# Gated cross-attention block: the context in pairs of tiles, the turn of the probabilities half a step earlier, row sums on ScalarE, side pieces at other places

## The reference, cut to what matters

```
x = x + tanh(g_xattn[0]) * xattn0(layernorm(x), ctx)     # 16 heads of 128, q and k RMS-normalised
x = x + tanh(g_ffn[0])   * mixture0(layernorm(x))        # dense layer and the best 2 of 8 low-rank experts
x = x + tanh(g_xattn[1]) * xattn1(layernorm(x), ctx)     # out = V @ sigmoid(Q^T K / sqrt(64)), Q = x, K = V = ctx
x = x + tanh(g_ffn[1])   * experts1(layernorm(x))        # the best 1 of 8 experts
```

```
q = rms_norm(x @ q_w + q_b, nq_s);  k = rms_norm(ctx @ ki_w + ki_b, nki_s);  v = ctx @ vi_w + vi_b
out = softmax(q k^T / sqrt(128)) v  per head and sequence;   xattn0 = out @ o_w + o_b
```

## Time and profile before

| | us |
|---|---|
| median of 3 runs | 1546.93 (1543.83 to 1551.09) |
| profiled execution, its own time | 1544.57 |
| its span, first to last instruction | 1542.8 |
| PE busy | 1419.3 (92%) |
| DVE busy | 976.3 (63%) |
| ACT busy | 599.5 (39%) |
| POOL busy | 63.8 (4%) |

### The profile page before, as it was taken

The page is one execution under the profiler, slowest core; times in us unless marked ns, Lnnn a source line. Parts: engine busy times, 40 slices in busy tenths (PEclk is TensorE's granted clock), DMA queues, the critical chain, the costliest instruction groups (busy, mean ns, idle before and its releaser), DMA issues.

```text
span 1542.8 us, 28633 instructions
## 1 busy us (share of the span) xinstructions
PE 1419.3 (92%) x10671; PEld 1224.8 (79%) x10671; DVE 976.3 (63%) x3000; ACT 599.5 (39%) x1065; POOL 63.8 (4%) x42
## 2 busy tenths in 40 slices
PE   7799999999999989999999999999899999999666
PEld 7688878788887978888887878879778888879545
DVE  6666677566775568565775667746686557746434
ACT  3344544434344343433434334443434434443221
POOL 2000000100010000100001000000001000000000
PEclk9999999999999999999999999999999999999858
DMA  7211411112112121112112121120211111220000
GB/s 267 76 62 69 151 56 43 69 55 96 42 56 69 42 84 55 58 55 96 56 42 69 55 84 48 64 69 32 94 55 56 55 69 56 69 69 17 25 0 14
DMA packets 48765, 100.31 MB, mean 65 GB/s; under 512 B 7569, under 2 KB 31345, under 8 KB 47985
## 3 DMA queue, kind: packets, MB, share of 16 engines
q1 hardware_dynamic: 48624, 98.38, 18.5%
HBM read 85.78 MB, written 12.58 MB: 64 GB/s over the span
## 4 chain that ended last, share of the span: by engine, by line
PE 67%; DVE 21%; issue 6%; ACT 4%; DMA 0%; SPq 0%; DVEq 0%; ACTq 0%
PE bank L116 44%; PE bank L897 7%; PE bank L999 4%; PE bank L908 3%; PE bank L874 3%; DVE pt L1299 3%; DVE stats L1341 2%; PE bank L888 2%; ACT ao_hi L633 2%; ACT xn L657 1%; DVE rmax L1316 1%; PE bank L1011 1%; PE bank L864 1%; DVE logit L1314 1%; DVE ao_lo L1306 1%
## 5 line engine op out<-in xcount | busy, mean ns | idle before, releaser
L644 ACT ACTIVATE k_sb<-bank,vecs 128x512 f32<-128x512 f32 x128 | 87.9, 687 | 341.2 <-PE bank L116 341.2
L1299 DVE COPY pt<-bank 64x128 f32<-64x128 f32 x512 | 147.4, 288 | 105.8 <-PE bank L888 94.9
L116 PE MATMUL bank<-so,ao_hi 128*128 128x256 f32 x1024 | 198.0, 292 | 2.9 <-DVE ao_lo L1306 2.9
L116 PE MATMUL bank<-sv,ct_hi 128*128 128x256 f32 x1024 | 197.8, 292 | 0.0
L1306 DVE SCALAR_TENSOR_TENSOR ao_lo<-bank,vecs,ao_hi 128x512 fp32r<-128x512 f32 x128 | 96.0, 750 | 151.3 <-ACT ao_hi L633 150.0
L897 PE MATMUL bank<-pt,v_sb 128*128 128x128 f32 x1024 | 140.1, 280 | 32.7 <-DVE pt L1299 32.6
L897 PEld LDWEIGHTS bank<-pt,v_sb 128*128 128x128 f32 x1024 | 127.3, 191 | 52.3 <-DVE pt L1299 41.6
L116 PEld LDWEIGHTS bank<-sv,ct_hi 128*128 128x128 f32 x1024 | 156.2, 189 | 12.8 <-issue 7.8
L116 PEld LDWEIGHTS bank<-so,ao_hi 128*128 128x128 f32 x1024 | 156.5, 190 | 3.3 <-issue 3.3
L116 PE MATMUL bank<-so,ao_lo 128*128 128x256 f32 x512 | 143.6, 280 | 0.0
L116 PE MATMUL bank<-sv,ct_lo 128*128 128x256 f32 x512 | 142.9, 279 | 0.0
(11 more groups left out here) (228 smaller groups left out, 2773.7 us busy)
## 6 DMA issues: line engine op xcount, KB each, us to landing
sv<-v_scratch SPq DMA_DIRECT2D x56, 512.0 KB, 3.2
so<-o_scratch SPq DMA_DIRECT2D x56, 512.0 KB, 3.2
cin<-in_ctx_dram SPq DMA_DIRECT2D x16, 512.0 KB, 4.9
xin<-in_x_dram SPq DMA_DIRECT2D x8, 512.0 KB, 4.9
xres<-in_x_dram SPq DMA_DIRECT2D x8, 512.0 KB, 5.0
v_scratch<-sv SPq DMA_DIRECT2D x8, 512.0 KB, 2.7
o_scratch<-so SPq DMA_DIRECT2D x8, 512.0 KB, 2.6
out_dram<-x SPq DMA_DIRECT2D x8, 512.0 KB, 3.0
```

What stands on the lines that cost most here:

```text
L116: last = pe.matmul(out, lhs[a], rhs[b], start=start and n == 0, stop=stop and n == 2, **kw)
L644: act.activation(k_sb[:, h % 2, :], bank[:, :], ACT.Identity, bias=vecs[:, 3 * H + h:3 * H + h + 1]).then_inc(pj_read.sem, 1)
L1299: last = dve.tensor_copy(pt[b * SEQ:(b + 1) * SEQ, q::2, b * SEQ:(b + 1) * SEQ], src[:, :, b * SEQ:(b + 1) * SEQ])
```

## The change

1. *Context by pairs of tiles.* `cin` is loaded by four DMAs, so that its tile (q, b) holds sequence b of token tiles 2q (partitions 0 to 63) and 2q + 1 (partitions 64 to 127). `keys(t, b)` finds the 64 columns of a sequence in this layout. The transposed probabilities of a pair of tiles then stand in the partitions that `pt` needs: two copies, 64 x 256 each, one on ACT (`prob_copy` there, rows 0 to 63) and one on DVE (rows 64 to 127). `attend` writes with a step, in the old token order.
2. *Turn half a step earlier.* `prob_transpose` is for head h - 2, writes `pv_ps`, and stands behind the scores; it waits for `ao_ready` of the head before. `attend` stands behind the output projection.
3. *Softmax.* `rr` carries a minus sign; DVE takes the row minimum (`least`), ACT computes exp(-x + least) per tile, four instructions, and sums the rows with them (`rsum`).
4. *The transposed context* is written to memory at step 3 (`keep_context`) and read back behind step 11 (`load_context`) in place of the transposes of `cin2`.
5. *Side pieces* have other places (`TURN_AT`, `GRAM_AT`, `AFF_AT` and `share`), `split` is in two parts, and two affinity pieces are issued together, alternating halves of the rows.
6. *GpSimd's additions* are four instructions of 128 x 256 each.

```diff
         def prob_transpose(g, h):
             pe.wait_ge(p_ready.sem, p_ready.count(g, h))
-            pe.wait_ge(l_ready.sem, l_ready.count(g, min(h + 1, -1) if is_body(g, NG) else h + 1))
+            ao_ready.wait(pe, g, h - 1)
             for q in range(2):
-                last = pe.transpose(at_ps[:, q * P:(q + 1) * P],
+                last = pe.transpose(pv_ps[:, q * P:(q + 1) * P],
...
         def attend(g, h):
-            pe.wait_ge(pt_ready.sem, pt_ready.count(g, h))
+            for half in pt_ready:
+                pe.wait_ge(half.sem, half.count(g, h))
             pe.wait_ge(pj_read.sem, pj_read.count(g, 3 * (h + 1 - h % 2) + 1))
-            ao_ready.wait(pe, g, h - 1)
...
+            dst = by_batch(pv_ps[:, :])
+            for q in range(2):
+                for i in range(2):
+                    last = pe.matmul(dst[:, q, i], v_sb[:, (h // 2) % 2, 2 * q + i, (h % 2) * HD:(h % 2 + 1) * HD],
+                                     pt[:, q, i, :], start=True, stop=True)
...
-        def affinity(b, j):
+        def affinity(b, t):
+            s, dst = b - 1, [take(b, "aff", 2 * t + i) for i in range(2)]
...
             for c in range(DC):
+                for i in range(2):
+                    rows = slice(i * SEQ, (i + 1) * SEQ)
+                    last = pe.matmul(dst[i][:, c * D:(c + 1) * D], xn[rows, t, c * P:(c + 1) * P], cin2[rows, t, :],
+                                     start=True, stop=True)
...
         def exps(g, h):
             act.wait_ge(l_ready.sem, l_ready.count(g, h))
-            act.activation(expo[:, :, :], logit[:, :, :], ACT.Exp).then_inc(e_ready.sem, 1)
+            for t in range(NT):
+                last = act.activation(expo[:, t, :], logit[:, t, :], ACT.Exp, scale=-1.0, bias=least[:, t:t + 1],
+                                      accum_out=rsum[:, t:t + 1])
+            last.then_inc(e_ready.sem, 1)
...
-            chain.link(dve.tensor_reduce(rmax[:, :], logit[:, :, :], AXX, ALU.max))
-            dve.tensor_tensor(logit[:, :, :], logit[:, :, :],
-                              rmax[:, :].unsqueeze(2).to_broadcast([P, NT, SEQ]),
-                              ALU.subtract).then_inc(l_ready.sem, 1)
+            dve.tensor_reduce(least[:, :], logit[:, :, :], AXX, ALU.min).then_inc(l_ready.sem, 1)
...
-            chain.link(dve.tensor_reduce(rsum[:, :], expo[:, :, :], AXX, ALU.add))
             chain.link(dve.reciprocal(rinv[:, :], rsum[:, :]))
...
+        def keep_context(g):
+            dst = turned_view(g)
+            sp.wait_ge(tr_read.sem, tr_read.count(g, NT - 1))
+            sp.dma_start(dst, cs[:, :, :].rearrange("p c n -> p (c n)")).then_inc(cs_kept.sem, 16)
...
+    AFF_AT = {(9, "b"): 0, (9, "c"): 1, (9, "d"): 2, (9, "e"): 3}
...
-                if at == (4, "d"):
+                if at == (8, "a"):
                     square_norms(n)
-                if at == (5, "b"):
+                if at == (12, "a"):
                     norm_factors()
...
-                if at == (8, "a"):
+                if at == (8, "e"):
                     later_normalise(s, 1, x2, xn2_ready)
```

More of the change, by code:

```diff
@@ L288, in layers @@
     xin_in = signal("xin_in", 16)
-    cin_in = signal("cin_in", 16)
+    cin_in = signal("cin_in", 64)
     xres_in = signal("xres_in", 16)
@@ L309, in layers @@
     pt_full = signal("pt_full", H)
-    pt_ready = signal("pt_ready", H)
+    pt_ready = [signal(f"pt_ready{i}", H) for i in range(2)]
     pv_full = signal("pv_full", H)
@@ L336, in layers @@
     cin2_in = signal("cin2_in", 16)
-    ct_full = signal("ct_full", 2)
-    ct_ready = signal("ct_ready", 2)
+    cs_kept = signal("cs_kept", 16)
+    ctf_in = signal("ctf_in", 16)
     csum_ready = signal("csum_ready", 1)
@@ L497, in body @@
                     load_residual(b)
-                if h == 9:
+                if h == 3 and not is_body(b, NG - 1):
+                    keep_context(b + 1)
+                if h == 11:
                     load_context(b)
@@ L566, in with_context_sum @@
             pool.wait_ge(csum_ready.sem, csum_ready.count(s, 0))
-            pool.tensor_tensor(x2[:, :, :], x2[:, :, :], csum[:, :].unsqueeze(2).to_broadcast([P, NT, D]),
-                               ALU.add).then_inc(x2c_ready.sem, 1)
+            for t in range(NT):
+                last = pool.tensor_tensor(x2[:, t, :], x2[:, t, :], csum[:, t:t + 1].to_broadcast([P, D]), ALU.add)
+            last.then_inc(x2c_ready.sem, 1)
         def body(b):
@@ L616, in transposed @@
             act.wait_ge(tr_full.sem, tr_full.count(g, t))
+            if t == 0:
+                cs_kept.wait(act, g - 1, 15)
             b = bank_of("tr", t)
@@ L753, in share @@
                     value_high(h // 2 + 1)
-                if p == "b" and h % 2:
+                if p == "c" and h % 2:
                     output_high((h - 1) // 2)
@@ L892, in attend @@
         def attend(g, h):
-            pe.wait_ge(pt_ready.sem, pt_ready.count(g, h))
+            for half in pt_ready:
+                pe.wait_ge(half.sem, half.count(g, h))
             pe.wait_ge(pj_read.sem, pj_read.count(g, 3 * (h + 1 - h % 2) + 1))
-            ao_ready.wait(pe, g, h - 1)
-            for t in range(NT):
-                last = pe.matmul(pv_ps[:, t * P:(t + 1) * P],
-                                 v_sb[:, (h // 2) % 2, t, (h % 2) * HD:(h % 2 + 1) * HD],
-                                 pt[:, t, :], start=True, stop=True)
+            dst = by_batch(pv_ps[:, :])
+            for q in range(2):
+                for i in range(2):
+                    last = pe.matmul(dst[:, q, i], v_sb[:, (h // 2) % 2, 2 * q + i, (h % 2) * HD:(h % 2 + 1) * HD],
+                                     pt[:, q, i, :], start=True, stop=True)
             last.then_inc(pv_full.sem, 1)
@@ L903, in scores @@
             pe.wait_ge(pj_read.sem, pj_read.count(g, 3 * h + 2))
-            pt_ready.wait(pe, g, h + 1 - ATT_LAG)
+            l_ready.wait(pe, g, h - 1)
             for t in range(NT):
@@ L991, in mixture @@
             last.then_inc(lora_full.sem, 1)
-        def affinity(b, j):
-            s, dst = b - 1, take(b, "aff", j)
-            t, rows = j // 2, slice(j % 2 * SEQ, (j % 2 + 1) * SEQ)
-            if j == 0:
+        def affinity(b, t):
+            s, dst = b - 1, [take(b, "aff", 2 * t + i) for i in range(2)]
+            if t == 0:
                 pe.wait_ge(xn2_ready.sem, xn2_ready.count(s, 0))
+                pe.wait_ge(cin2_in.sem, cin2_in.count(s, 15))
             for c in range(DC):
-                last = pe.matmul(dst[:, c * D:(c + 1) * D], xn[rows, t, c * P:(c + 1) * P], cin2[rows, t, :],
-                                 start=True, stop=True)
-            last.then_inc(aff_full.sem, 1)
+                for i in range(2):
+                    rows = slice(i * SEQ, (i + 1) * SEQ)
+                    last = pe.matmul(dst[i][:, c * D:(c + 1) * D], xn[rows, t, c * P:(c + 1) * P], cin2[rows, t, :],
+                                     start=True, stop=True)
+                    if c == DC - 1:
+                        last.then_inc(aff_full.sem, 1)
         def second_attention(b, j):
             s, dst = b - 1, take(b, "att", j)
-            pe.wait_ge(ct_ready.sem, ct_ready.count(s, j))
+            pe.wait_ge(ctf_in.sem, ctf_in.count(s, 15))
             pe.wait_ge(th_ready.sem, th_ready.count(s, 4 * j + 3))
@@ L1009, in second_attention @@
                     for i in range(2):
-                        tok = (2 * j + t) * P + i * SEQ
-                        last = pe.matmul(dst[i * SEQ:(i + 1) * SEQ, t * D:(t + 1) * D], ct[:, c, tok:tok + SEQ],
+                        last = pe.matmul(dst[i * SEQ:(i + 1) * SEQ, t * D:(t + 1) * D], ct[:, c, keys(2 * j + t, i)],
                                          th[:, 4 * j + 2 * t + i, c, :], start=c == 0, stop=c == DC - 1)
@@ L1597, in _ @@
         gram_sums(0, 1)
-        split(0)
+        split(0, 0)
+        split(0, 1)
         value_low(0)
@@ L1643, in build @@
                *(a["L0_ffn_" + n] for n in ("W", "b", "lora_A", "lora_B", "gate_w", "gate_b")),
-               *(a["L1_ffn_" + n] for n in ("A", "Bw", "Wg")), out, v_dram, o_dram)
+               *(a["L1_ffn_" + n] for n in ("A", "Bw", "Wg")), out, v_dram, o_dram, c_dram)
 def kernel(**inputs):
```

318 lines of the change are left out of this document (155 added, 163 removed).

## The result

The changed kernel takes 1486.9 us (median of four runs, 1485.3 to 1489.0) where the kernel before took 1549.0 beside it (1543.8 to 1552.9): a ratio of 0.960, 95% interval 0.957 to 0.964. On another chip, later, it was 0.9575 (0.955 to 0.960).

The account below looks back on a forecast made before the run. TensorE, busy 92% of the span, was taken as the bound. From 1544.6 us: 45.7 less work, +5.0 waits, +3.4 clock gave 1507.3; 2.4 up to the median made 1510. Range 1490 to 1534.

Parts of the forecast that it names:

- affinity in pairs: Affinity pieces of seven groups, two issued together on alternating row halves: 1.01 us a pair, 39.5 us saved.
- context transposes: Two transpose pieces a group go, the transposed context being read back from memory: 6.2 us saved.
- ordinary blocks of a step: TensorE's plain step of 7.54 us: the sum had no term for its becoming shorter, so 0.
- waits: TensorE's idle time over all groups, old waits removed against new ones: +5.0 us together.
- clock: TensorE's clock: new waits of 2.1 and 2.4 us add two falls to half, +3.4 us.
- Rival D: Better: waits of steps 0 and 9 partly hidden and fewer clock falls, 1491 us; chance 0.15.
- Rival B: Affinity passes in pairs don't overlap: 35 us come back, 1545 us; chance 0.04.
- group 0, first transposes: Transposes waited 4.78 us for the first normalisation; score factors and logits ahead of the scales add 3.4.
- step 2: The next group's transposes wait 1.3 us (was 0.7) for the normalisation, moved behind the exponentials.
- step 5: ao_hi stands behind the normalisation of step 4: a wait of 0.35 us.
- step 9, with its neighbours: Affinity pairs wait: first 2.4 us for normalisation, second 0.6 for both banks, fourth 0.4 behind exponentials and a copy.
- step 12: Normalisation behind the scales of step 11, then the transpose behind ao_lo: 1.6 us of wait (was 1.1).

Follow-up runs that it names:

- Attend back in front of the scores: The changed kernel with attend back directly ahead of the scores, its copies behind the k copy: one execution, 1594.4 us, own time 1342.9 us.

## Why the prediction was wrong

Its sum, term by term, against the profiled execution:

| term | forecast | measured |
|---|---|---|
| affinity in pairs | -39.5 | -32.7 (alone, in the kernel before) |
| context transposes | -6.2 | -6.8 (their records in the trace; not run alone) |
| ordinary blocks of a step | 0 | -14.2 (8.6 of it by the plain step) |
| waits | +5.0 | +1.9 |
| clock | +3.4 | -3.9 |

**The step that failed most** is the first paragraph's: "What can be won is TensorE work taken out, and waits taken out." (That ScalarE and VectorE can't shorten a plain step, the sentence before it, holds.) The change also puts the same blocks in another order, and the prediction set that at nothing without a reason: it had the plain step from the earlier trace rows and never asked what a new neighbour costs. Measured, it is 14.2 us. A plain step is 0.067 us shorter, 8.6 us over 128 heads, and the blocks' table under "Attend back in front of the scores" puts this at the transpose: directly behind it output takes 1.51 us, k 1.48 and q 1.47, against 1.39 to 1.41 behind v, q, k or output, while v takes 1.49 behind it and 1.51 behind the scores. Between scores and v the transpose itself takes 0.05 us more, but makes no neighbour dearer. One place later, behind v, it costs 0.04 of the 0.067 again. Attend's new place is worth nothing in a plain step. Why a block behind the transpose is longer is not shown, and some 6 of the 14.2 us, about the scatter of own time, lie in steps with side pieces and stay without a cause.

**The clock** was forecast with the wrong sign. The prediction took a fall for the price of a gap of about 2 us and added two. Measured, a gap of 2.5 us in step 9 (once 3.2) stands in both the changed kernel and the one with the loop written out, in six groups each; a fall comes with it once in the one and six times in the other. Over the runs there were between 0 (pairs alone) and 11 falls (transpose behind values) from 100 us to the last group, with no order by the sum of waits. What does hold: the four kernels that took 9.1, 10.8, 11.0 and 16.3 us of idle time out of the changed one lost 5.6 to 10.1 us more to the clock, and over all their executions the granted clock was 0.960 to 0.972, against 0.970 to 0.975. Why is open. Rival D had fewer falls in it and the time nearest to the result (1491), but its other half, hidden waits, did not happen. From five falls, with 1.7 us each, the term is a range from 8 us less to some 10 more; +3.4 was no more than a point in it.

**The pairs** were mis-sized: 1.01 us a pair, from passes 0.108 us apart. They start two by two, 0.204 to 0.216 us apart, which is the pace that the four passes of a single piece had; the row of the last group (2.08 at half clock, so 1.04) gave the right value and had been left for the lower one. With the change-over a pair costs 1.15 to 1.26 (in the kernel with the pairs alone, steps of 11.00 us with three and of 10.05 with two, over 7.54), about what a piece did. Rival B, no overlap, falls. This error worked against the others: without it the forecast would have been 5 to 7 us further off.

**The waits** came nearly as long as forecast, and most of them where:

| place | forecast | measured (looped group) |
|---|---|---|
| group 0, first transposes | 8.2 | 8.29 |
| step 2 | 1.3 | 1.16 |
| step 5 | 0.35 | none |
| step 9, with its neighbours | 3.4 (2.4, 0.6, 0.4) | 3.4 (2.54 and 0.18; 0.36 and 0.31 in step 8) |
| step 12 | 1.6 | 1.16 |
| top of a group, without the jump's gap | 2.1 | 1.76 (1.04, 0.72) |

That step 9 comes out at 3.4 is partly luck: the first pair's wait was right, the other two were not, and two that nobody forecast fill their place. Missed were the last group, where idle time grew by 3.6 in place of nothing (three waits of 1.23 us for the second bank, and 8.07 in place of 6.37 for the first normalised tile), and in the other direction groups 1 and 2, where it fell by 4.3 us (from 8.5 and 10.8 to 7.5 and 7.4) in place of growing by 0.8: the kernel before had waited 1.7 and 1.9 us there in step 2, not the 0.7 of the group that was read, and the changed one has the shorter waits of the table. In groups 3 to 6 it fell by 1.6, forecast 0.8. Attend's waits went but for 1.9 us; of the other signs that the prediction named, the affinity line came to 41.0 (under 40 expected) and TensorE's busy time to 57 less (45). ScalarE's four exponentials:

```profile
791.14 0.35 ACT L684 ACTIVATE expo<-logit,least 128x64 f32<-128x64 f32 x1 [3.62 <-DVE least L1342]
791.40 0.19 ACT L684 ACTIVATION_READ_ACCUMULATOR expo<-logit,least 128x1 f32 x1
791.49 0.33 ACT L684 ACTIVATE expo<-logit,least 128x64 f32<-128x64 f32 x1
...
792.48 0.57 ACT L700 ACTIVATE v_sb<-bank 128x512 f32<-128x512 f32 x1
```

1.34 us from the first to the next work, against 1.4 taken. The estimate by the Trainium skill ("ScalarE: Activation LUTs", What ACT_TABLE_LOAD costs) was 1.05: it has no row for a sum as second output, and the trace shows a second instruction for each.

**The rest** is that the profiled execution of before was taken as 2.4 us under its median. Against the four runs it is 4.4 under, and the changed kernel's is 2.1 over: 6.5 us of the medians' difference are not in the two traces.

## What to carry to other kernels

Where one engine is 92% busy, its own time is not fixed by the list of its instructions: count what each block costs behind its new neighbour, by whole steps and not by blocks, and move one block back to see it. A block moved back that brings waits with it tells little about its place. Passes on different halves of the rows need not alternate, if the row on each half is short: four and four overlapped here, eight and eight only in part. A microsecond of idle time removed is not a microsecond won as long as the clock moves: compare kernels by idle time, own time and clock apart, over several executions.

## What the hardware showed that was not expected

- Four passes on rows 0 to 63 and four on rows 64 to 127 run side by side even when written one set after the other (1.07 us either way); with eight and eight passes of 64 columns, the second half starts after five of the first (0.90 us in place of 0.62).
- At the ends of a row of half-width passes the starts lie further apart: scores 0.058 us apart, then 0.160 to the transpose; the second pair of affinity passes 0.308 behind the first, then 0.204. That this is the change-over's price is a reading, no run varies it alone.
- A projection or output block directly behind the transpose takes 0.07 to 0.11 us more (1.47 to 1.51 in place of 1.40); behind the scores the transpose costs v nothing.
- A GpSimd addition of 2.41 us holds one small VectorE operation for 2.26 us where the two meet; in quarters two operations take 0.56 and 0.67.
- Jumping back in the loop costs TensorE 1.7 to 4.2 us a turn inside the first scores, from one turn to the next of the same execution; with the loop written out the gap is gone.
- Executions of the kernel before differ by 13 us on one chip (20 on another), and about half of it goes with the granted clock.
